# Graph attention on one core: the mixing matmuls of a pair of tiles move from the middle of a slot to behind the scores

## The reference, cut to what matters

```python
q = heads(x @ Wq + bq); k = heads(x @ Wk + bk); v = heads(x @ Wv + bv)
scores = jnp.einsum('bhqd,bhkd->bhqk', q, k) * scale
scores = jnp.where(mask[:, None] == 0, -jnp.inf, scores)
attn = jax.nn.softmax(scores, axis=-1)
out = jnp.einsum('bhqk,bhkd->bhqd', attn, v)
out = out.transpose(0, 2, 1, 3).reshape(b, s, D_MODEL)
return layernorm(x + out @ Wo + bo)
```

## Time and profile before

| | |
|---|---|
| time, median of 3 runs | 811.19 us (809.91 to 812.51) |
| time of the profiled execution | 811.64 us |
| its span, first to last instruction | 809.5 us |
| TensorE busy | 800.8 us, 99% of the span |
| VectorE, GpSimd, ScalarE busy | 642.8, 551.4, 267.1 us |

### The profile page before, as it was taken

One profiled execution on the slowest core, in us unless ns is written; L12 is line 12 of the kernel. 1 busy time (PEld: TensorE's weight loads), 2 busy tenths in 40 slices (PEclk: granted clock), 3 DMA queues, 4 the chain that ended last, 5 costly groups with the idle time before them and its releaser, 6 DMA issues.

```text
span 809.5 us, 26951 instructions
## 1 busy us (share of the span) xinstructions
PE 800.8 (99%) x11771; PEld 679.1 (84%) x11771; DVE 642.8 (79%) x1002; ACT 267.1 (33%) x349; POOL 551.4 (68%) x443
## 2 busy tenths in 40 slices
PE   9999999999999999999999999999999999999997
PEld 7778888888888888888888888888888888888876
DVE  5968778787778887887877788877878777876895
ACT  6533333323333223332233332233322333323223
POOL 1797778666687666786667767667866668755672
PEclk9999999999999999999999999999999999999999
DMA  9334545254352534534345344444435435234342
GB/s 330 125 80 121 162 119 160 84 154 142 106 183 79 161 118 119 177 98 142 115 114 177 115 129 124 146 146 117 156 88 163 122 116 176 75 105 117 96 107 103
DMA packets 64965, 106.62 MB, mean 132 GB/s; under 512 B 11728, under 2 KB 28624, under 8 KB 62672
## 3 DMA queue, kind: packets, MB, share of 16 engines
q1 hardware_dynamic: 52368, 87.85, 34.7%
q10 hardware_dynamic: 12480, 17.06, 8.1%
HBM read 54.53 MB, written 16.78 MB: 88 GB/s over the span
## 4 chain that ended last, share of the span: by engine, by line
PE 93%; DVE 2%; DMA 2%; POOL 1%; SPq 1%; issue 0%; ACT 0%; POOLq 0%; DVEq 0%
PE ring L367 15%; PE ring L369 14%; PE ring L368 14%; PE ring L519 7%; PE ring L520 7%; PE ring L523 7%; PE psum_s L470 6%; PE psum_s L440 6%; PE ring L461 6%; PE psum_s L472 6%; PE psum_s L474 6%; DMA x_raw<-in_xt 2%; DVE x_lo L885 0%; DVE wo_lo L1014 0%; POOL soft L232 0%; POOL soft L1178 0%
## 5 line engine op out<-in xcount | busy, mean ns | idle before, releaser
L1178 POOL TENSOR_TENSOR soft<-soft,top 128x1024 f32<-128x1024 f32 x62 | 123.4, 1991 | 22.1 <-DVE top L950 22.1
L232 POOL TENSOR_TENSOR soft<-soft,inverse 128x1024 f32<-128x1024 f32 x62 | 118.8, 1918 | 25.9 <-DVE inverse L957 25.8
L954 DVE TENSOR_REDUCE total<-soft 128x16 f32<-128x1024 f32 x62 | 75.2, 1213 | 48.8 <-ACT soft L713 48.8
L367 PE MATMUL ring<-x_hi,wk_hi 128*128 128x512 f32 x256 | 103.2, 403 | 1.6 <-DVE v L891 1.3
L713 ACT ACTIVATE soft<-soft 128x1024 f32<-128x1024 f32 x62 | 65.8, 1062 | 111.6 <-POOL soft L1178 111.6
L369 PE MATMUL ring<-x_hi,wk_lo 128*128 128x512 f32 x256 | 99.9, 390 | 0.0
L368 PE MATMUL ring<-x_lo,wk_hi 128*128 128x512 f32 x256 | 99.7, 389 | 0.0
L519 PE MATMUL ring<-wo_hi,ot_hi 128*128 128x512 f32 x252 | 99.1, 393 | 0.0
L520 PE MATMUL ring<-wo_lo,ot_hi 128*128 128x512 f32 x252 | 98.9, 392 | 0.0
L748 ACT CAST s_hi<-v 128x1024 fp32r<-128x1024 f32 x27 | 28.3, 1047 | 207.4 <-DVE v L903 207.4
L367 PE MATMUL ring<-x_hi,wq_hi 128*128 128x512 f32 x248 | 96.6, 389 | 0.0
(11 more groups left out here) (125 smaller groups left out, 1878.2 us busy)
## 6 DMA issues: line engine op xcount, KB each, us to landing
pt<-soft SPq DMA_DIRECT2D x248, 64.0 KB, 2.5
x_raw<-in_xt SPq DMA_DIRECT2D x15, 1024.0 KB, 6.8
row<-in_x SPq DMA_DIRECT2D x60, 256.0 KB, 2.7
out_rows<-row SPq DMA_DIRECT2D x60, 256.0 KB, 2.4
pt<-soft ACTq DMA_DIRECT2D x232, 64.0 KB, 2.3
v<-in_xt SPq DMA_DIRECT2D x27, 512.0 KB, 4.6
adj<-in_adj SPq DMA_DIRECT2D x16, 128.0 KB, 2.7
kt<-in_wk SPq DMA_DIRECT2D x4, 256.0 KB, 5.7
```

Of the source, the lines that this page charges most:

```text
L232: ops.tensor_tensor(soft_of(c), soft_of(c), on_keys(inverse[:, c % 2, :]), ALU.mult).then_inc(normed, 1)
L367: nc.tensor.matmul(out, left_hi, right_hi, start=kc == 0, stop=False)
L954: nc.vector.tensor_reduce(total[:, c % 2, :], by_row_head(soft_of(c)), AX_XY, ALU.add).then_inc(summed, 1)
L1178: nc.gpsimd.tensor_tensor(soft_of(c), soft_of(c), on_keys(top[:, c % 2, :]), ALU.subtract).then_inc(centred, 1)
```

## The change

In slots p >= 2 the mixing of the pair in front, with its wait for `row_added`, moves from behind the four projections to directly behind the two scores. Slot 1 keeps the old place for pair 0, and the part written out by hand is unchanged. SP gets a wait on that mixing before `store(a - 3)`.

```diff
@@ SP
                 if p >= 2:
+
+                    sp.wait_ge(mixed, 2 * p)
                     store(a - 3)
                 load_row(b)
@@ TensorE
                 if p == 1:
                     pe.wait_ge(v_done, 1)
                 else:
+
                     score(a)
                     score(b)
+                    wait_for(pe, row_added, a - 2)
+                    mix(a - 2)
+                    mix(b - 2)
                     pe.wait_ge(k_done, a + 4)
                 project_k(a + 4)
...
                 pe.wait_ge(q_done, a + 5)
                 project_q(b + 4)
-                wait_for(pe, row_added, a - 2)
-                mix(a - 2)
-                mix(b - 2)
+                if p == 1:
+                    mix(0)
+                    mix(1)
                 first_products(p)
```

## The result

| | before | after |
|---|---|---|
| median time | 810.68 us (809.91 to 812.51, 4 runs) | 870.04 us (867.73 to 870.22, 4 runs) |
| ratio | 1 | 1.0723, 95% interval 1.0702 to 1.0743 |
| span of the profiled execution | 809.5 us | 868.3 us |
| 26 changed slots, from the scores of slot 2 to the first scores behind the loop | 643.76 us | 701.74 us |

The change costs 59 us, 7.2%. The direction was forecast, the size was not: 845 us was forecast, and the range ended at 866. All but 1 us of the 58.8 us by which the span grew lies in the 26 changed slots.

The account below looks back on a forecast made before the run. TensorE, busy 800.8 of 809.5 us, was taken to bound the kernel. From the profiled execution's 811.6 us, 38 us of stalls were added and 26 x 0.2 us of saved edges subtracted, giving 845 us, range 806 to 866.

Parts of the forecast that it names:

- The second code block inside a burst: In the merged scores and mix, TensorE reaches a second block edge before its code arrives: 21 x 1.8 = 38 us.
- in a list of all 92 no two are closer: Code queue's packets: two 3.6 us apart are the closest, taken as second witness that a block needs 3.6 us.
- the saving: In each changed slot, burst edges vanish when mix follows scores: at most 0.20 us a slot, 5.2 us in all.
- one slot in five: Share of changed slots whose first edge lies at the head of the scores and lose nothing, leaving 21 stalled.
- I take 1.8: Stall in a merged burst, in us, chosen between bounds of 1.4 and 2.2 for the unknown lead of instructions.
- I expect it to stay there: TensorE's granted clock in the slot: expected to stay at 1.00, the 2.4 GHz level; no time added.
- The floor of 24.56: Shortest slot, in us, set by the row_added loop through mix, projections, first products and VectorE, with 0.05 latency.
- The stalled case: Code stalls in merged bursts, the likeliest case, chance 0.72: 845 us, own range 821 to 872.
- the faster rival: Code arrives in time in merged bursts because the refill reads several blocks ahead: 806 us, chance 0.15.
- the later read_ot: In each slot read_ot follows read_q, so split_ot slides some 0.5 us with 0.6 to spare: costs nothing.
- the probabilities: Transposed probabilities land before the mix, costing nothing; the rival with them 2 us late: 819 us, chance 0.04.
- no change: Rival: code in time, but the scores-mix seam and the row_added wait eat the saving: 811 us, chance 0.09.

Follow-up runs that it names:

- shift40: The changed kernel with 40 empty semaphore increments on TensorE ahead of its first projection; 865.52 us in one run.
- lock_worst: The changed kernel with 22 empty increments in every slot p >= 2, between second and third projection, making a slot 768 instructions; 865.28 us.
- lock_best2: The changed kernel with spread empty increments: 70 in seven groups in the opening and slot 1, then 6, 6, 5 and 5 per slot; 809.67 us.
- no_sp: The changed kernel without SP's new wait on the mix; 866.96 us.
- part: The changed kernel with the first half of one K projection (1.36 us) between scores and mix, the second half behind the mix; 829.03 us.
- lock_best: The changed kernel with 22 empty increments in every slot p >= 2 and 72 more ahead of the first projection; 827.20 us.

## Why the prediction was wrong

**The mechanism was right.** "The second code block inside a burst" is what costs the time; shift40, lock_worst and lock_best2 show it. The signs named in advance came: "issue" rows before L463, packets of the code queue 3.7 us apart in a slot with a halt. In the changed kernel's slot from 640.31 the two stretches of 0.4 us from 641.1 and 644.8 each hold one; their rows in the view of the DMA queues (packets, MB, share of the 16 engines):

```profile
q8 instruction: 1, 0.02, 15.7%
...
q8 instruction: 1, 0.02, 26.5%
```

TensorE's timeline in between, where it goes on at 643.80:

```profile
643.80 1.29 PE L463 MATMUL ring<-pt,v 64*32 64x64 f32 x106 [1.47 <-issue]
```

The second packet comes after the halt, which fits a block that is asked for when the one before it begins. That answers to the earlier trace rows.

One witness was misread: "in a list of all 92 no two are closer" than 3.6 us. In the kernel before, the packets in the 0.4 us from 321.4 and from 324.7 lie 3.3 us apart:

```profile
q8 instruction: 1, 0.02, 14.5%
...
q8 instruction: 1, 0.02, 19.9%
```

The 3.6 us is no fixed length either. In lock_worst the edge falls at the scores' 49th matmul, and the mix goes on 3.07 to 4.05 us after that matmul's start.

**Three terms of the sum were too small, and the saving too large.** The 26 slots grew by 58 us, made up so:

- *Number of halts.* I put "one slot in five" at an edge that loses nothing and took 21 stalled slots. There were 25, and one free. An early first edge is not enough: with edges 16 instructions into the scores (slot 10) the next one but one falls 14 instructions behind the burst and halts the first projection there for 0.62 us, and with 46 (slot 23) the mix halts for 1.47. No halt showed with edges 20, 24, 26 and 28 instructions into the scores (shift40's slots from 347.18 and 666.17, the free slot here, lock_best2). I had not followed the third edge.
- *Length of a halt.* "I take 1.8" was for the lead with which instructions are sent ahead. The idle rows of the loop sum to 43.7 - 1.05 + 2.0 + 0.6 = 45.3 us, 1.8 a halt. But a halted slot at the full clock is some 0.2 us longer than its idle row (26.66 - 24.64 - 1.80 = 0.22): idle time is counted only from the recorded end of the matmul before, 0.23 us after its start. So a halt costs 2.04 us, 25 x 2.04 = 51, where I had 38.
- *The clock.* "I expect it to stay there" is the step that failed outright; it had a price of nothing. Seven of the 26 slots ran part of the time at the 1.2 GHz level and took 27.8 to 28.9 us; beyond their halts that is 1.2 to 1.7 us each, about 10 us. The prediction said that idle stretches of 2 us are not in the trace, and still took the cheap end of that unknown.
- *The saving.* A slot without a halt takes 24.64 us, 0.12 less than before, where I had 0.20. The floor of 24.56 had a latency of 0.05 us from add_y(a-3) to the mix in it, read from a weight load behind ot_lo. In the free slot add_y(a-3) ends at 616.45 + 0.68 = 617.13 and the mix starts at 617.28, 0.15 us later:

```profile
615.67 1.59 PE L442 MATMUL psum_s<-kt,qt 32*64 32x64 f32 x128
616.45 0.68 DVE L985 TENSOR_TENSOR row<-ring,row 128x512 f32<-128x512 f32 x1
617.28 1.47 PE L463 MATMUL ring<-pt,v 64*32 64x64 f32 x128
```

In the trace TensorE's wait there is over 0.04 us after add_y(a-3) ends, in all 26 slots, and the first mix matmul starts 0.11 us after that (0.29 in slot 21). So the mix does hang on row_added; with 0.15 for 0.05 the floor is 24.66 us, and 24.64 was measured. 26 x 0.12 = 3 us.

51 + 10 - 3 = 58. With the forecast terms, 38 - 5 = 33. Of the 25 us between them 13 lie in the halts, 10 in the clock and 2 in the saving. The stalled case's own range, 821 to 872, held the measured 870; the range given ended at 866, because it was moved down towards the faster rival.

**What held.** SP's wait, the later read_ot, the probabilities and load_pair cost nothing that shows (no_sp; TensorE's waits name none of them). The mechanism of the faster rival, a refill that reads several blocks ahead, is out: TensorE would not halt at the edges then. Its time comes near when the edges are moved: lock_best2's 809.7 us lies between that rival's 806 and the 811 of "no change". The Trainium skill, Runtime: NRT & Kernel Launch, section Instruction fetch mechanics, gives TensorE room for 2048 instructions and calls the fetch hidden; the 25 halts do not agree. Its remark in the same section that the store has only two lines of 16 KiB does agree with a block that is asked for only when the one before it begins.

## What to carry to other kernels

Count instructions as well as time. A block of 256 instructions took 3.1 to 4.1 us to come here (lock_worst), and 256 short matmul and weight-load instructions in a row last 1.4 us; where two block edges fall into one such run, TensorE can halt for the difference. Put long matmuls between short bursts (2.7 us of them were enough here, 1.36 us were not), or, if bursts must touch, check where the block edges fall. When a forecast holds a halt of a couple of microseconds on TensorE, price the granted clock behind it too: it fell in 7 of 26 slots in the changed kernel and in 6 of 26 in lock_worst.

## What the runs showed of the hardware

- The halts repeat by instruction count: 22 instructions more in a slot of 746 made them stand still for 26 slots, and 40 more ahead of the loop moved them by 20 short matmuls.
- At the same edge the idle time varied from 1.30 to 2.28 us and the time from that edge to the next block's first matmul from 3.07 to 4.05 us (lock_worst), so a block's arrival is not of fixed length; what else moves at that time was not tried.
- The length of a halt alone doesn't decide whether the clock falls. In the changed kernel it went to the 1.2 GHz level at the halt of 2.53 us that ends at 269.57 and at that of 1.69 us that ends at 347.84, and stayed at the 2.4 GHz level at that of 2.52 us that ends at 161.26. In part, whose halts are 1.0 us at most, it did not fall in the loop.
- An empty semaphore increment on TensorE is not free: in a row one starts 0.15 us after the other (lock_best). It costs time where TensorE has too little work queued to cover it: 22 in a slot delayed a projection in lock_best and none in lock_worst.
